# Two-layer graph network on one core: the node block's load moved behind the first feature load, and VectorE's per-tile duties moved to other tiles

## Chip, cores and metric

The kernel runs on one core of a Trainium2 chip. The metric is the device time of one execution in microseconds (us); the figure to compare is the median of the runs.

## What is computed

The graph has 6250 nodes with 256 features and 206250 edges, sorted by destination. The reference is two layers with a residual and a layer norm around each (cut to what matters here):

```python
# layer 0: every edge sends from src to dst
msg = concat([x[src], edge_attr_64]) @ W_message
agg = segment_sum(msg, dst)
h   = layer_norm(relu(agg) + x)
y   = relu_mlp_skip(h, [W0, W1, W2], [b0, b1, b2])
x1  = norm(x + layer_norm(x + y))
# layer 1: attention over the edges of one src
h      = lrelu(x1 @ w_W + w_b)
edge_h = lrelu(edge_attr_128 @ ew_W + ew_b)
e_ij   = concat([h[src], h[dst], edge_h]) @ a_W + a_b
alpha  = softmax of e_ij over the edges of one src
out    = norm(x1 + lrelu(segment_sum(alpha * h[dst], src)))
```

## The kernel before

After a short stage that prepares tables, the first long stage is a loop of 51 passes that ends near 2900 us of the span; the second long stage, the attention over sorted records, is not touched. The change concerns the pass loop alone.

One pass works on 32 tiles (numbered `kk` = 0 to 31) of 128 edges. For each tile TensorE multiplies the 128 edge features by `w_edge` (line 657) into a PSUM bank that ScalarE has filled with the bias beforehand (`seed`, line 801), and VectorE reduces the bank to one logit per edge (`edge`, line 1034). ScalarE seeds tile `kk + 3` while at tile `kk`, and a bank can be seeded only when VectorE has read the tile that used it before, four or five tiles back (nine for the fifth bank). TensorE asks for two seeds at every even tile.

Beside that, each pass carries four other jobs, spread over its tiles:

- **Segment sums of layer 0.** GpSimd gathers node rows with 35 indirect transfers (line 624, in eight batches that `picked` indexes), VectorE builds one-hot matrices `hot` (`one_hot`, line 1060), TensorE adds them up from tile 3 to tile 30 (line 672), and VectorE takes the sum at tile 30 (`take_sums`, line 1068).
- **The node block.** One block of 128 nodes goes through layer 0's dense part. `x_blk` is loaded by SyncE's queue (`load_x`, line 591), VectorE adds it (line 1090), the three MLP layers alternate between TensorE (line 731) and VectorE (lines 1107 and 1109, tiles 12, 15 and 18), two norms follow (tiles 21 to 25), `last_norm` writes `x1` as `u_n` (line 1128, tile 25), TensorE turns it at tile 28 (line 723) and multiplies it at tile 30 (`hidden`, line 751), and VectorE makes the table row from that (`table`, from line 1134, tile 30).
- **Sorting the edges by src,** for layer 1. VectorE computes ranks, writes one-hot `slot` matrices in four parts (`slots`, line 995) and `tagged` values: three parts from the keys (`tag_keys`, line 1006) in this pass and three from the logits (`tag_logits`, line 1024) at tiles 0 to 2 of the next. TensorE sorts from tile 4 of that next pass (line 696).
- **Loads.** SyncE's queue loads edge features in eight pieces of four tiles into two halves of `feats` (line 600) and 64-wide edge rows (line 604). A feature piece waits until the half's four tiles of earlier use are multiplied.

Each engine runs its own instructions in the order in which they are written, so the tile at which a duty stands in `body` sets what is queued behind it. At a pass's start SyncE first calls `load_x`, which waits for the `x1` of the previous pass.

Of the kernel before, what the change touches and what calls it, by code (L numbers as in the profile page):

```python
# [58 lines left out]
def build(nc, a, n_nodes, n_edges):  # L59
# [24 lines left out]
    with ExitStack() as top:  # L84
# [25 lines left out]
        def wait_alone(eng, *waits):  # L110
            waits = [(on, eng.to_reg(count)) for on, count in waits]
            eng.wait_ge(opened, 1)
            for on, count in waits:
                eng.wait_ge(on, count)


        def in_pairs(t):
            return t.rearrange("p t (c w) -> p t c w", w=2)

        def pairs_over(row, many):  # L120
            pairs = row.rearrange("p (c w) -> p c w", w=2)
            return pairs.unsqueeze(1).to_broadcast([P, many, row.shape[1] // 2, 2])

        def over_pairs(two, wide):
            return two.unsqueeze(2).to_broadcast([P, two.shape[1], wide // 2, 2])
# [37 lines left out]
        with ExitStack() as ctx:  # L163
# [70 lines left out]
            @block.sync  # L234
            def _(sp):
                sp.dma_start(dst_g[:], a["dst_groups"]).then_inc(idx_in, 16)
                sp.dma_start(dst_i[:], a["dst"]).then_inc(idx_in, 16)
                sp.dma_start(hi_i[:], a["src"]).then_inc(idx_in, 16)
                sp.dma_start(src_i[:], a["src"][:, 0:NTA]).then_inc(idx_in, 16)

                sp.wait_ge(blank_ready, 1)
                for n in range(2):
                    sp.dma_start(recs[n * SPAN:(n + 1) * SPAN, :].rearrange("(p t) w -> p (t w)", p=P), blank[:]).then_inc(blanked, 16)
                sp.wait_ge(blanked, 2 * 16)
# [213 lines left out]
        with ExitStack() as ctx:  # L458
# [96 lines left out]
            def count_of(eng):  # L555
                return eng.value_load(passes[0:1, 0:1], min_val=EP, max_val=NPM - 1)

            def block_at(eng, p):
                return eng.value_load(block_i[:, bass.ds(p, 1)], min_val=0, max_val=NB)

            def tile_at(eng, p):
                return eng.value_load(tile_i[:, bass.ds(p, 1)], min_val=0, max_val=USED)

            def edges_at(eng, p):
                return eng.value_load(edges_i[:, bass.ds(p, 1)], min_val=0, max_val=EP + 1)

            @block.sync
            def _(sp):
                def load(dst, src):
                    sp.dma_start(dst, src).then_inc(w_in, 16)  # L570

                load(w_edge[:, 0:D], a["ew_W"])
                for n, name in enumerate(("a_tgt", "a_nbr", "a_edge")):
                    load(row[name], a["a_W"][n:n + 1, :].to_broadcast([P, D]))
                for name in ("w_b", "ew_b", "aggr_scale", "aggr_bias", "out_scale", "out_bias"):
                    load(row[name], a[name].to_broadcast([P, D]))
                load(ab_col[:], a["a_b"].to_broadcast([P, 1]))
                for c in range(KC):
                    load(w_msg[:, c, :], a["W_message"][c * P:(c + 1) * P, :])
                    load(w_node[:, c, :], a["w_W"][c * P:(c + 1) * P, :])  # L580
                    for n in range(3):
                        load(w_mlp[:, n, c, :], a[f"mlp_W{n}"][c * P:(c + 1) * P, :])
                load(w_msg[0:DE0, KC, :], a["W_message"][D:D + DE0, :])
                for n in range(3):
                    load(b_mlp[:, n, :], a[f"mlp_b{n}"])

                def load_x(p):

                    sp.wait_ge(nx["x1"], p)
                    d = block_at(sp, p)  # L590
                    sp.dma_start(x_blk[:], a["x"][bass.ds(d * P, P), :]).then_inc(nx["x"], 16)

                n = count_of(sp)
                with sp.Fori(0, n) as p:
                    load_x(p)
                    e = edges_at(sp, p)
                    t0 = tile_at(sp, p)
                    for c in range(TILES // EB):
                        sp.wait_ge(o["y_ready"], p * TILES + (c * EB - EB + Y0))
                        sp.dma_start(feats[:, c % 2 * EB * P:(c % 2 + 1) * EB * P],  # L600
                                     a["edge128"][:, bass.ds(e * (TILES * P) + c * EB * P, EB * P)]).then_inc(f_in[c % 2], 16)
                        j, at = c, STARTS[c]
                        sp.wait_ge(o["summed"], p * NB_SUMS + (j + 1))
                        sp.dma_start(rows[:, at:at + SUMS[j], D:W0], a["edge64"][:, bass.ds(t0 + at, SUMS[j]), :]).then_inc(e_in[j], 16)
                load_x(n)
                wait_alone(sp, (nx["tab_out"], n * 16 + 16))

# [287 lines left out]
            def _(dve):  # L895
# [95 lines left out]
                def slots(p, n):  # L991
                    if n == 0:
                        wait_alone(dve, (o["ranked"], p * 2 + 2), (o["sorted"], p * U + U))
                    tiles = slice(n * SLOT_TILES, (n + 1) * SLOT_TILES)
                    v.tensor_tensor(in_pairs(slot[:, tiles, :]), pairs_over(one_up[:], SLOT_TILES), over_pairs(rank_two[:, tiles, :], P),
                                    ALU.is_equal).then_inc(o["slot_ready"], 1)
# [5 lines left out]
                def tag_keys(p, n):  # L1002

                    if n == 0:
                        wait_alone(dve, (o["keys_ready"], p + 1), (o["hb_ready"], p + 1), (o["sorted"], p * U + U))
                    v.tensor_tensor(in_pairs(tagged[:, :, n, 0, :]), in_pairs(hb[:]), over_pairs(key_two[:, n, :, :], NBP), ALU.mult)
# [16 lines left out]
                def tag_logits(w, n):  # L1023
                    ins = v.tensor_tensor(in_pairs(tagged[:, :, n, 1, :]), in_pairs(hb[:]), over_pairs(r_two[:, n, :, :], NBP), ALU.mult)  # L1024
                    if n == 2:
                        ins.then_inc(o["tagged_ready"], 1)
# [122 lines left out]
                def body(p, e, tile):  # L1149
                    at = e * TILES  # L1150
                    split_logits(p, at)
                    for kk in range(TILES):
                        edge(p, kk)
                        if kk < 3:
                            tag_logits(p, kk)
                        if kk == 3:
                            find(p, at)
                        if 4 <= kk < 7:
                            totals(p, kk - 4)
                        if kk in (7, 8):  # L1160
                            in_lane(p, kk - 7, at)
                        if kk in (9, 10):
                            up_to_here(p, kk - 9)
                        if kk in (9, 13):
                            place(p, (9, 13).index(kk), e)
                        if kk == 10:
                            key_pairs(p, at)
                        if kk in (12, 13):
                            look_up(p, kk - 12)
                        if kk == 14:  # L1170
                            halve(p)
                        if kk == 15:
                            halve_again(p)
                        if kk == 16:
                            rank_of(p)
                        if kk == 17:
                            rank_pairs(p)
                        if kk in (18, 21, 23, 27):
                            slots(p, (18, 21, 23, 27).index(kk))
                        if kk in (19, 25, 29):  # L1180
                            tag_keys(p, (19, 25, 29).index(kk))
                        if kk in hot_at:
                            one_hot(p, hot_at[kk])
                        if kk in pick_at:
                            pick(p + 1, pick_at[kk], tile)
                        if kk in node:
                            node[kk](p)
                        if kk == 24:
                            base_of(p + 1)
                            go_on(p)  # L1190
                        if kk == 25:
                            local(p + 1, tile)
                        if kk == 26:
                            one_hot(p + 1, 0)
                        if kk == 28:
                            one_hot(p + 1, 1)
                        if kk == 30:
                            take_sums(p)
# [635 lines left out]
```

## Time and profile before

| | |
|---|---|
| median of 3 runs | 5291.64 us (5288.85 to 5291.9) |
| the profiled execution: time, span | 5291.46 us, 5289.7 us |
| mean granted TensorE clock | 0.892 |
| TensorE matmul / VectorE / GpSimd busy | 74% / 67% / 68% |
| the pass loop | 51 passes; the VectorE instruction that opens a pass starts at 208.7 us the first time |

The profiled execution's span is 1.8 us under its time. Shares of busy time are means over two stages with different limits; the loop is read below from its own rows.

### The profile page before, as it was taken

What the parts mean: (1) busy time and instruction counts of PE and PEld (TensorE: products, weight loads), DVE (VectorE), ACT (ScalarE), POOL (GpSimd) and SP (SyncE); (2) the same over time, 40 slices, a digit from 0 to 9 for tenths busy, and PEclk for the clock granted to TensorE, in tenths of its full rate; (3) what the DMA queues carried; (4) which work ended last, traced back from release to release, by engine and by line L of the source; (5) the groups of instructions that cost most, each with busy time, mean ns of one, the idle gap of its engine ahead of it and who ended that gap; (6) DMA issues with size and microseconds to landing.
All of it is one profiled execution on the core that took longest, in us unless ns stands there. A gap on an engine that the chain in (4) does not pass through costs nothing. (4 is left out here: it accounts for less than half of the span.)

```text
span 5289.7 us, 86818 instructions
## 1 busy us (share of the span) xinstructions
PE 3902.5 (74%) x18662; PEld 2967.3 (56%) x18663; DVE 3563.6 (67%) x11443; ACT 1726.2 (33%) x5121; POOL 3584.2 (68%) x3655
## 2 busy tenths in 40 slices
PE   4498989898989898988887366666666666666661
PEld 3366666666666666666665255555555555555551
DVE  8778888888888888888786455555555555555554
ACT  0133333232323333333332133333333333333334
POOL 0377776777777777777773277777777777777772
PEclk9799999999999999999998688888888888888886
DMA  1356555555555555555556334344444334433343
GB/s 44 96 164 170 158 164 154 165 155 161 157 162 157 160 157 160 157 162 160 157 164 94 101 107 106 106 106 106 106 106 106 106 106 105 107 106 106 106 105 64
DMA packets 544286, 679.76 MB, mean 129 GB/s; under 512 B 340246, under 2 KB 376430, under 8 KB 543996
## 3 DMA queue, kind: packets, MB, share of 16 engines
q0 software_dynamic: 174144, 469.02, 32.6%
q1 hardware_dynamic: 355132, 196.63, 13.8%
q10 hardware_dynamic: 14976, 13.69, 0.8%
q8 instruction: 18, 0.29, 0.0%
q14 instruction: 16, 0.13, 0.0%
HBM read 650.32 MB, written 27.79 MB: 128 GB/s over the span
## 5 line engine op out<-in xcount | busy, mean ns | idle before, releaser
L624 POOL DMA_INDIRECT rows<-in_x,picked x1785 | 1799.1, 1008 | 724.1 <-issue 686.0
L1499 POOL DMA_INDIRECT room<-nodetab,nbr_idx x1736 | 1643.8, 947 | 562.4 <-issue 490.2
L672 PE MATMUL bank<-rows,hot 128*128 128x320 f32 x3570 | 1237.5, 446 | 25.7 <-DMA rows<-in_edge 19.7
L657 PE MATMUL bank<-w_edge,feats 128*128 128x258 f32 x3264 | 1050.6, 411 | 213.0 <-DMA feats<-in_edge 108.7
L801 ACT COPY bank<-b_edge 128x258 f32<-128x258 f32 x1635 | 602.7, 377 | 1460.6 <-DVE unused L1034 1442.9
L1529 PE MATMUL bank<-room,w 128*128 128x258 f32 x3472 | 1037.9, 462 | 51.2 <-ACT w L1575 50.7
L1561 ACT ACTIVATE w<-off,logit 128x128 f32<-128x128 bf16 x1736 | 534.0, 388 | 1361.0 <-DVE logit L1613 1361.0
L1529 PEld LDWEIGHTS bank<-room,w 128*128 128x128 f32 x3472 | 802.8, 238 | 244.4 <-ACT w L1575 95.0
L1520 PE MATMUL bank<-ident,w 128*128 128x128 f32 x1736 | 307.4, 330 | 777.2 <-ACT w L1561 777.2
L657 PEld LDWEIGHTS bank<-w_edge,feats 128*128 128x128 f32 x3264 | 578.7, 200 | 433.3 <-ACT bank L801 197.6
L1034 DVE SCALAR_TENSOR_TENSOR unused<-bank,a_relu 128x258 bf16<-128x258 f32 x1632 | 687.5, 421 | 199.2 <-PE bank L657 173.6
L672 PEld LDWEIGHTS bank<-rows,hot 128*128 128x128 f32 x3570 | 704.7, 198 | 179.9 <-issue 41.9
L1520 PEld LDWEIGHTS bank<-ident,w 128*128 128x128 f32 x1736 | 233.3, 166 | 824.0 <-ACT w L1561 437.0
L1618 DVE TENSOR_REDUCE best<-bank 128x1 f32<-128x896 f32 x248 | 270.7, 1091 | 475.0 <-PE bank L1520 474.9
L1613 DVE TENSOR_TENSOR logit<-r_at,room 128x7 f32<-128x7 f32 x248 | 42.4, 171 | 455.4 <-DMA room<-nodetab,nbr_idx 454.6
L1608 DVE TENSOR_SCALAR off<-iota_bf,lane_f 128x128 bf16<-128x128 bf16 x1736 | 337.8, 276 | 1.6 <-issue 1.6
L696 PE MATMUL bank<-tagged,slot 128*128 128x300 bf16 x1664 | 283.5, 293 | 54.9 <-DVE tagged L1024 54.6
L1637 DVE TENSOR_TENSOR w<-w,bank 128x896 f32<-128x896 f32 x248 | 268.5, 1083 | 58.2 <-PE bank L1512 55.3
L1060 DVE TENSOR_TENSOR hot<-iota,rel 128x512 f32<-128x512 f32 (+1 forms) x410 | 300.8, 734 | 0.1
L696 PEld LDWEIGHTS bank<-tagged,slot 128*128 128x128 bf16 x1664 | 159.4, 98 | 198.6 <-issue 143.0
L1575 ACT ACTIVATE w<-w 128x896 f32<-128x896 f32 x248 | 231.7, 934 | 4.4 <-DVE w L1637 4.4
L617 POOL DMA_INDIRECT recs<-out_rows,at_now x106 | 107.3, 1012 | 111.9 <-ACT out_rows L815 80.9
(316 smaller groups left out, 3871.4 us busy)
## 6 DMA issues: line engine op xcount, KB each, us to landing
feats<-in_edge SPq DMA_DIRECT2D x408, 256.0 KB, 2.9
rows<-in_edge SPq DMA_DIRECT2D x255, 128.0 KB, 3.0
rows<-in_x,picked POOLq DMA_INDIRECT x1785, 2.9
room<-nodetab,nbr_idx POOLq DMA_INDIRECT x1736
rows<-in_edge SPq DMA_DIRECT2D x153, 160.0 KB, 3.4
nodetab<-tab ACTq DMA_DIRECT2D x52, 129.0 KB, 2.7
x_blk<-in_x SPq DMA_DIRECT2D x52, 128.0 KB, 2.1
x_rows<-u_n ACTq DMA_DIRECT2D x52, 128.0 KB, 2.3
```

The lines of the kernel that those rows point to most:

```text
L624: pool.indirect_dma_start(out=rows[:, STARTS[j] + s, 0:D], out_offset=None, in_=a["x"], in_offset=bass.IndirectOffsetOnAxis(ap=picked[j][: ...
L657: mm(y, feats[:, f0 * P:(f0 + 1) * P], w_edge[:], start=False, stop=True, skip_group_check=True).then_inc(o["y_ready"], 1)
L672: ins = mm(S_PS, hot[j % HR][:, s - STARTS[j], :], rows[:, s, :], start=(s == 0), stop=(s == SA - 1), skip_group_check=True)
L696: ins = mm(SORT, slot[:, at, :], tagged[:, at, :, :, :].rearrange("p n f b -> p (n f b)"), start=(t == 0), stop=(t == L - 1), skip_group_c ...
L801: s.copy(logits_of(kk), b_edge[:]).then_inc(o["seeded"], 1)
L1034: v.scalar_tensor_tensor(unused[:, kk % EB, :], logits_of(kk), 0.0, a_relu[:], ALU.max, ALU.mult, accum_out=r_cur[:, kk:kk + 1]).then_inc( ...
L1060: v.tensor_tensor(hot[j % HR][:, 0:SUMS[j], :], iota[:].unsqueeze(1).to_broadcast(shape), rel[:, at:at + SUMS[j]].unsqueeze(2).to_broadcas ...
L1499: pool.indirect_dma_start(out=nbr[:, u * GC + k, :], out_offset=None, in_=nodetab, in_offset=bass.IndirectOffsetOnAxis(ap=nbr_idx[u][:, k: ...
L1520: ins = nc.tensor.transpose(T_PS[u % 2][:, k * P:(k + 1) * P], w[:, u * GC + k, :], ident[:])
L1529: ins = mm(O_PS[u % 2][:, 0:HW], w[:, u * GC + k, :], nbr[:, u * GC + k, :], start=(k == 0), stop=(k == GC - 1))
L1561: ins = s.activation(w[:, u * GC + k, :], off[:, u * GC + k, :], ACT.Identity, bias=logit[u][:, k:k + 1])
L1608: v.tensor_scalar(off[:, u * GC + k, :], iota_bf[:], lane_f[:, bass.ds(tile0(i, u) + k, 1)], MASKED, ALU.not_equal, ALU.mult)
```

## The change

It does two things. In SyncE's queue `load_x(p)` moves from the head of the pass to behind the pass's first feature and row transfers. On VectorE the same instructions stand at other tiles: `slots` at 18, 21, 26, 28 (before 18, 21, 23, 27), `tag_keys` at 17, 20, 25 (before 19, 25, 29), `base_of` and `go_on` at 22 (before 24), `local` at 23 (before 25), and the next pass's first two `one_hot` at 24 and 27 (before 26 and 28). No instruction is added or taken away.

```diff
                 with sp.Fori(0, n) as p:
-                    load_x(p)
                     e = edges_at(sp, p)
                     t0 = tile_at(sp, p)
                     for c in range(TILES // EB):
...
                         sp.dma_start(rows[:, at:at + SUMS[j], D:W0], a["edge64"][:, bass.ds(t0 + at, SUMS[j]), :]).then_inc(e_in[j], 16)
+                        if c == 0:
+                            load_x(p)
                 load_x(n)
...
-                        if kk in (18, 21, 23, 27):
-                            slots(p, (18, 21, 23, 27).index(kk))
-                        if kk in (19, 25, 29):
-                            tag_keys(p, (19, 25, 29).index(kk))
+                        if kk in (18, 21, 26, 28):
+                            slots(p, (18, 21, 26, 28).index(kk))
+                        if kk in (17, 20, 25):
+                            tag_keys(p, (17, 20, 25).index(kk))
...
-                        if kk == 24:
+                        if kk == 22:
                             base_of(p + 1)
                             go_on(p)
-                        if kk == 25:
+                        if kk == 23:
                             local(p + 1, tile)
-                        if kk == 26:
+                        if kk == 24:
                             one_hot(p + 1, 0)
-                        if kk == 28:
+                        if kk == 27:
                             one_hot(p + 1, 1)
```

The changed kernel's lines below the first edit are numbered one higher, so L1109 of before is L1110 there.

VectorE, tiles 17 to 19 of a pass, before: the logit of tile 17 (L1034), the rank pairs, the logit of tile 18, a quarter of `slot`, the residual of MLP layer 2 (L1109), the logit of tile 19, and then the first `tag_keys` (L1006).

```order
L1034 SCALAR_TENSOR_TENSOR unused,r_cur<-bank,a_relu 128x258
L987 COPY rank_two<-rank 128x64
L1033 REGISTER_ALU
L1034 SCALAR_TENSOR_TENSOR unused,r_cur<-bank,a_relu 128x258
L995 TENSOR_TENSOR slot<-one_up,rank_two 128x1024
L1109 SCALAR_TENSOR_TENSOR h_t<-bank,b_mlp,h_t 128x128 x2
L1033 REGISTER_ALU
L1034 SCALAR_TENSOR_TENSOR unused,r_cur<-bank,a_relu 128x258
L1006 TENSOR_TENSOR tagged<-hb,key_two 128x32x50
L1057 REGISTER_ALU
L1060 TENSOR_TENSOR hot<-iota,rel 128x512
```

The same place in the changed kernel:

```order
L1035 SCALAR_TENSOR_TENSOR unused,r_cur<-bank,a_relu 128x258
L988 COPY rank_two<-rank 128x64
L1007 TENSOR_TENSOR tagged<-hb,key_two 128x32x50
L1034 REGISTER_ALU
L1035 SCALAR_TENSOR_TENSOR unused,r_cur<-bank,a_relu 128x258
L996 TENSOR_TENSOR slot<-one_up,rank_two 128x1024
L1110 SCALAR_TENSOR_TENSOR h_t<-bank,b_mlp,h_t 128x128 x2
L1034 REGISTER_ALU
L1035 SCALAR_TENSOR_TENSOR unused,r_cur<-bank,a_relu 128x258
L1058 REGISTER_ALU
L1061 TENSOR_TENSOR hot<-iota,rel 128x512
```

The first `tag_keys` now stands ahead of the residual of layer 2 and not behind it.

VectorE from the logit of tile 25 to `x1` (L1128), before:

```order
L1034 SCALAR_TENSOR_TENSOR unused,r_cur<-bank,a_relu 128x258
L1006 TENSOR_TENSOR tagged<-hb,key_two 128x32x50
L1040 REGISTER_ALU
L1041 ISA
L1041 COPY picked<-src_i 128x4
L1084 REGISTER_ALU
L1085 RECIPROCAL rstd<-std 128x1
L111 REGISTER_ALU
L1128 TENSOR_SCALAR u_n<-u,mv,rstd 128x256
```

In the changed kernel, from the logit of tile 24 to `x1` (L1129 there):

```order
L1035 SCALAR_TENSOR_TENSOR unused,r_cur<-bank,a_relu 128x258
L1061 TENSOR_TENSOR hot<-iota,rel 128x640
L1034 REGISTER_ALU
L1035 SCALAR_TENSOR_TENSOR unused,r_cur<-bank,a_relu 128x258
L1007 TENSOR_TENSOR tagged<-hb,key_two 128x32x50
L1041 REGISTER_ALU
L1042 ISA
L1042 COPY picked<-src_i 128x4
L1085 REGISTER_ALU
L1086 RECIPROCAL rstd<-std 128x1
L111 REGISTER_ALU
L1129 TENSOR_SCALAR u_n<-u,mv,rstd 128x256
```

The tag there is now the third, not the second, and the next pass's first one-hot (L1061) stands ahead of it.

SyncE's queue at the head of a pass, before: the node block's load with its register load, then the two other register loads, then the first features.

```order
L559 TENSOR_LOAD pass_tab
L559 ISA x2
L591 ISA
L591 DMA x_blk<-in_x 128x256
L565 ISA
L565 TENSOR_LOAD pass_tab
L565 ISA x2
L562 ISA
L562 TENSOR_LOAD pass_tab
L562 ISA x2
L599 ISA
L600 ISA
```

In the changed kernel:

```order
L599 ISA
L599 DMA feats<-in_edge 128x512
L602 ISA
L603 ISA
L603 DMA rows<-in_edge 128x5x64
L559 ISA
L559 TENSOR_LOAD pass_tab
L559 ISA x2
L591 ISA
L591 DMA x_blk<-in_x 128x256
L598 REGISTER_ALU
L599 ISA
```

The wait for `x1` (the ISA row of L559) and the node block's transfer now stand behind the first features and rows.

## Rows read from the trace of the kernel before

**Rows 1.** Waits, 500 to 2500 us: total us, times, longest.
```profile
PE bank L657 <- DMA feats<-in_edge: 73.6, 38, 3.0
DVE h_t L1109 <- PE bank L731: 15.2, 39, 0.4
```

**Rows 2.** Timeline of VectorE, tiles 15 to 18: start, us, line, [idle before].
```profile
1024.85 0.61 DVE L1107 SCALAR_TENSOR_TENSOR h_t<-bank,b_low,s_t 128x128 f32<-128x128 f32 x2 [1.59 <-PE bank L731]
...
1027.81 0.69 DVE L995 TENSOR_TENSOR slot<-one_up,rank_two 128x1024 bf16<-128x1024 bf16 x1
1028.88 0.61 DVE L1109 SCALAR_TENSOR_TENSOR h_t<-bank,b_mlp,h_t 128x128 f32<-128x128 f32 x2 [0.39 <-PE bank L731]
```

**Rows 3.** Timeline of VectorE, tile 25 to the next pass's opening.
```profile
1039.34 0.99 DVE L1006 TENSOR_TENSOR tagged<-hb,key_two 128x1600 bf16<-128x1600 bf16 x1
1040.24 0.16 DVE L1041 COPY picked<-src_i 128x4 int32 x1
...
1040.57 0.41 DVE L1128 TENSOR_SCALAR u_n<-u,mv,rstd 128x256 f32<-128x256 f32 x1
1040.90 0.37 DVE L1048 TENSOR_SCALAR rel<-dst_f,base_cur 128x35 f32 x1
1041.46 0.43 DVE L1034 SCALAR_TENSOR_TENSOR unused<-bank,a_relu 128x258 bf16<-128x258 f32 x1 [0.19 <-DVE rel L1048]
...
1041.82 0.82 DVE L1060 TENSOR_TENSOR hot<-iota,rel 128x640 f32<-128x640 f32 x1
1042.55 0.42 DVE L1034 SCALAR_TENSOR_TENSOR unused<-bank,a_relu 128x258 bf16<-128x258 f32 x1
...
1046.25 0.42 DVE L1134 TENSOR_TENSOR u<-bank,row_w_b 128x256 f32<-128x256 f32 x1
...
1051.59 0.19 DVE L1014 TENSOR_TENSOR r_rest<-r_cur 128x32 f32<-128x32 f32 x1 [1.88 <-issue]
```

**Rows 4.** Timeline of TensorE, tiles 28 to 30 and the next pass's 0 to 3.
```profile
1039.91 0.70 PE L657 MATMUL bank<-w_edge,feats 128*128 128x258 f32 x2 [0.47 <-ACT bank L801]
...
1041.04 0.44 PE L723 MATMUL bank<-ident,u_n 128*128 128x128 f32 x2
...
1042.67 0.70 PE L657 MATMUL bank<-w_edge,feats 128*128 128x258 f32 x2 [0.22 <-ACT bank L801]
...
1043.75 1.13 PE L751 MATMUL bank<-w_node,h_t 128*128 128x256 f32 x4
...
1047.61 1.13 PE L657 MATMUL bank<-w_edge,feats 128*128 128x258 f32 x4 [2.30 <-DMA feats<-in_edge]
1050.01 2.09 PE L657 MATMUL bank<-w_edge,feats 128*128 128x258 f32 x4 [1.27 <-ACT bank L801]
```

**Rows 5.** Timelines of SyncE's queue and ScalarE there; the seeds are tiles 3 and 4.
```profile
1041.82 0.34 SPq L591 DMA_DIRECT2D x_blk<-in_x  x1
1044.06 0.33 SPq L600 DMA_DIRECT2D feats<-in_edge  x1
...
1049.58 0.68 ACT L801 COPY bank<-b_edge 128x258 f32<-128x258 f32 x2
```

**Rows 6.** Windows around two pass heads: busy us of each engine, granted clock, DMA.
```profile
1724.00:1738.00 14.00, 7.74 (x34) 5.08 (x34) 11.26 (x38) 3.70 (x11) 10.87 (x11) 1.00 0.72 208
1045.00:1059.00 14.00, 10.26 (x36) 6.95 (x35) 11.21 (x37) 3.33 (x10) 10.65 (x12) 0.76 0.73 206
```

**Rows 7.** Timelines: openings of two later passes (VectorE), TensorE's first sort between.
```profile
1731.56 0.19 DVE L1014 TENSOR_TENSOR r_rest<-r_cur 128x32 f32<-128x32 f32 x1 [1.83 <-issue]
...
1736.50 0.69 PE L696 MATMUL bank<-tagged,slot 128*128 128x300 bf16 x4 [1.93 <-DVE tagged L1024]
...
1783.86 0.19 DVE L1014 TENSOR_TENSOR r_rest<-r_cur 128x32 f32<-128x32 f32 x1 [1.81 <-issue]
```

**Rows 8.** Timelines: opening after the pass of rows 3, and GpSimd's wait in a pass.
```profile
1103.87 0.19 DVE L1014 TENSOR_TENSOR r_rest<-r_cur 128x32 f32<-128x32 f32 x1 [1.83 <-issue]
...
1014.13 0.95 POOL L624 DMA_INDIRECT rows<-in_x,picked  x1 [4.04 <-issue]
```

## The prediction

> **What bounds the kernel now.** I read the waits first, then one pass on each engine, then the same place in other passes. The waits between 500 and 2500 us, 38 passes, show TensorE waiting 73.6 us for features: 1.9 us at every pass's head, because the feature load stands behind the node block's load in SyncE's queue [rows 1, 4, 5]. They also show VectorE waiting for TensorE ahead of the MLP's layer 2: 15.2 us, 0.39 us a pass [rows 1].
>
> Which of these sets the pass? One pass lasts 1103.87 - 1051.59 = 52.28 us from opening to opening [rows 3, 8]. VectorE waits 1.59 us for layer 1 at 1024.85 and 0.39 us for layer 2 at 1028.88 [rows 2]. After 1028.88 it waits for nobody: up to the opening of the next pass at 1051.59 it has only short gaps for its own results (0.19 us before the logit of tile 26) and the 1.88 us of the loop's own turn [rows 3]. It then makes the logit tags, and TensorE's first sort waits for them, 1.93 us in the pass of rows 7. From that sort TensorE runs densely until layer 2 (the waits list no wait of its own in that stretch, and VectorE is the one that waits). So the cycle is: VectorE from layer 2's residual to the logit tags, then TensorE from the first sort to layer 2. A wait counts only if it lies on that cycle.
>
> The feature wait does not. TensorE's multiply of tiles 0 and 1 starts at 1047.61; the one of tiles 2 and 3 starts at 1050.01 whatever happened before it, as it waits for ScalarE's seed of tile 3, which ends at 1049.58 + 0.38 (half of the 0.68 us pair, its second copy being tile 4's) [rows 4, 5]. That seed stands behind ScalarE's duty for the table, which waits for VectorE. And behind tiles 2 and 3 there is one more wait for VectorE, the sort's.
>
> The clock is a second candidate. In the pass head at 1045 to 1059 us the granted clock is 0.76 on average, so 0.24/0.5 x 14 = 6.7 us were at the lower level, 1.2 GHz: four matmuls took 2.09 us there, against 1.13 at the higher level, 2.4 GHz [rows 4, 6]. But another head, 1724 to 1738 us, had 1.00 throughout, and its pass took 1783.86 - 1731.56 = 52.30 us, the same; the sort merely waited 1.93 us [rows 6, 7].
>
> **The change, part by part.**
>
> *SyncE's queue.* The first features now wait only for tile 27's multiply and not for `x1`. Before, `x_blk` is issued at 1041.82, the features at 1044.06, and they are used at 1047.61, 3.55 us later [rows 4, 5]. Tile 27 is multiplied before 1039.91 minus the 0.47 us wait, so the features are issued near 1039.5 at the latest and there by 1043.1, ahead of 1047.61 - 2.30 = 1045.31, when TensorE asks. The feature wait, 1.9 us, goes. What is late next is the seed of tile 3: TensorE does tiles 0 and 1 about 1.7 us earlier and then waits so much longer. Worth: 0 us on the cycle. The seed wait and the sort wait are the cover; were both gone it would be worth up to 1.9 us a pass. `x_blk` itself leaves when `x1` is there, as before, and is wanted only at tile 5 of the next pass; queued behind it are the second features, which wait for tile 31 anyway (near 1045.3). One register load fewer stands before the first features, and none is added.
>
> *VectorE, the tag at tile 17.* A `tag_keys` takes 1040.24 - 1039.34 = 0.90 us in the stream [rows 3]. Moved ahead of layer 2's residual, it fills the wait there. A `slot` quarter takes 0.69 - 0.09 = 0.60 us in the stream (the tag's own row overlaps its follower by the same 0.09), so before, VectorE could have gone on at 1027.81 + 0.60 = 1028.41 and went on at 1028.88: 0.47 us were idle [rows 2]. With the tag ahead the residual starts at 1028.41 + 0.90 = 1029.31, which is 0.43 us later, and everything behind it finds 0.90 us less in front. Net: 0.47 us a pass earlier. TensorE doesn't want that residual until tile 21.
>
> *The other moves.* The second tag goes from 25 to 20, the third from 29 to 25, two `slot` quarters one to three tiles later, `base_of`, `go_on`, `local` and two one-hots earlier. All of them stay between the residual and `table`, where VectorE has no idle time to fill, so their sum is 0 us as long as nothing in that stretch begins to wait. Three places could:
> - `x1` comes later. Between residual and `x1` there are still two tags, but `local` (1041.46 - 1040.90 = 0.56 us) and a 640-wide one-hot (1042.55 - 1041.82 = 0.73) replace a `slot` quarter (0.60): +0.69 us, with the residual's 0.43 +1.1 us, so `x1` starts at 1041.7 and not 1040.57 [rows 3].
> - TensorE turns `x1` 0.47 us after that start (1041.04 against 1040.57), and `hidden` ended at 1043.75 + 1.13 = 1044.88, 3.84 us after the turn. In this lies a wait for a seed ahead of tile 30 (0.22 us idle at 1042.67) that a later `x1` swallows: 3.6 us remain, and `hidden` ends at 1041.7 + 0.47 + 3.6 = 1045.8 [rows 3, 4].
> - `table` wants `hidden`. It started at 1046.25 and would now be free to start at 1046.25 - 0.47 = 1045.78 [rows 3]. So nothing is left, within my 0.2 us of reading. If `hidden` is late by 0.2 us, nearly half the gain goes; I take it as late by 0 to 0.1.
>
> Seeds for tiles 28 and 29 also come later, as logits 24 and 25 do: TensorE's 0.47 us wait at tile 28 grows to about 1.5 us [rows 4]. It is off the cycle: it is inside the chain through `x1` just counted.
>
> *Sum.* 0.47 us in about 50 of 51 passes: 23.5 us. The second stage is unchanged. I take off 4 us for passes in which the clock falls at a worse place than now (below): 19.5 us. On the profiled execution's 5291.46 us (its span 5289.7 and 1.8 around it; 0.2 us under the median of the runs, 5291.64) that is **5272 us**.
>
> **The skill's rule.** The row shows that a clock fall follows the idle time at the pass head, and that a pass without one is no shorter [rows 6, 7]. The Trainium skill, "TensorE: Matmul & The Clock Gate", section "HAM oscillation — how this bites in real kernels", says that a wait for a transfer in every round of a loop puts TensorE back to the slow clock each time and that the cost is the slow time times one half. By that rule the load's move alone would return 6.7 x 0.5 = 3.4 us of such a pass. That is the first rival.
>
> **The rivals.**
> 1. *The feature wait and the clock count after all* (chance 0.10). If TensorE's head were on the cycle, 1.9 us a pass would come back, 95 us, and up to 3.4 us more with the clock. But GpSimd then becomes the bound: it waits 4.04 us a pass now [rows 8], so no pass can get shorter by more than that. Time: 5197, at the very least 5090. Against it stand the two passes of equal length with and without slow clock.
> 2. *No measurable change* (0.24). `hidden` is late for `table` by 0.3 us or more, or a logit in the stretch behind the residual, where VectorE had nothing to wait for, now waits. Each takes 0.2 to 0.4 us of the 0.47. Time: 5291.5 - 50 x 0.1 = 5286.
> 3. *Slower: the clock falls in the dense stretch* (0.09). Now it falls in the head, where half speed costs nothing, as two waits cover it. With TensorE working steadily at tiles 31, 0 and 1 the fall can miss the head and come at the wait for the sort, 1.93 us long when the clock is full [rows 7], and so reach into the stretch behind the sort, which is on the cycle. Half speed for the 6.7 us of rows 6, of which 3 to 5 behind the sort, costs 1.5 to 2.5 us in such a pass. It decides from about one pass in four (0.25 x 2 = 0.5 against 0.47). In every second pass it would give 5291.5 + 50 x (1.0 - 0.47) = 5318. For it: the sum of idle time stays, so a fall has to come somewhere. Against it: the seed wait of about 2.5 us stays in the head and is longer than the sort's wait. I expect one or two such passes in fifty: the 4 us above.
>
> **How the numbers follow.** The forecast case, a gain of 0.3 to 0.5 us a pass, has 0.57: 5264 to 5280. A measurement of this kernel can tell about 0.2%, 10.6 us, from no change. Below 5281 lie the forecast and rival 1: 0.67. Between lies rival 2: 0.24. Above lies rival 3: 0.09. The range leaves out rival 1 and most of rival 3; it goes from 5254 (0.75 us a pass, should a part of the head's 1.9 us count) to 5290.
>
> **What the changed profile would show.** The wait of TensorE for the features is gone; its wait for ScalarE before tiles 2 and 3 is near 2.6 us. VectorE's wait before layer 2's residual (L1110) is gone; the one at layer 1 is still near 1.6. Pass openings are 51.8 us apart. The wait at tile 28 is near 1.5 us. `table` (L1135) has no wait for TensorE; one there is rival 2. Windows behind the first sort have the clock at 1.00; below that is rival 3. The prediction is wrong if openings are 50 us apart or less, or more than 52.3.

## The result and the profile after

The changed kernel takes 5319.97 us, the median of 12 runs (5299.84 to 5366.29), against 5291.45 (5283.25 to 5293.06) for the kernel before. The ratio estimated from the runs is 1.0066, 95% interval 1.0047 to 1.0085 (the medians alone give 1.0054). It is slower, and its runs spread over 66 us where those of before spread over 10. The profiled execution is the fastest of the twelve, 5299.84 us with a span of 5298.1.

Waits of the changed kernel between 500 and 2500 us (total us, times, longest):

```profile
PE bank L658 <- ACT bank L802: 181.6, 97, 2.8
DVE h_t L1108 <- PE bank L732: 71.3, 70, 1.6
PE bank L697 <- DVE tagged L1025: 63.6, 37, 1.9
DVE u L1091 <- PE bank L719: 63.4, 38, 3.5
```

TensorE's wait for the features is gone from the list, and so is VectorE's wait ahead of layer 2's residual (L1110): neither row of [rows 1] is left. A wait that was short has grown: VectorE ahead of the node block's first sum (L1091), tile 5, 63.4 us and up to 3.5 at a time. Before the change the same view showed for it

```profile
DVE u L1090 <- PE bank L718: 22.9, 38, 0.6
```

One pass of the changed kernel that went as forecast, timeline of VectorE (start, us, line, idle before):

```profile
1158.04 0.19 DVE L1015 TENSOR_TENSOR r_rest<-r_cur 128x32 f32<-128x32 f32 x1 [2.04 <-issue]
1166.78 0.42 DVE L1091 SCALAR_TENSOR_TENSOR u<-bank,x_blk 128x256 f32<-128x256 f32 x1 [0.60 <-PE bank L719]
1183.63 0.61 DVE L1108 SCALAR_TENSOR_TENSOR h_t<-bank,b_low,s_t 128x128 f32<-128x128 f32 x2 [1.59 <-PE bank L732]
1188.09 0.61 DVE L1110 SCALAR_TENSOR_TENSOR h_t<-bank,b_mlp,h_t 128x128 f32<-128x128 f32 x2
1204.47 0.42 DVE L1135 TENSOR_TENSOR u<-bank,row_w_b 128x256 f32<-128x256 f32 x1
1209.88 0.19 DVE L1015 TENSOR_TENSOR r_rest<-r_cur 128x32 f32<-128x32 f32 x1 [1.95 <-issue]
```

And TensorE in it, at tile 28 and at tiles 2 and 3 of the next pass:

```profile
1199.73 0.70 PE L658 MATMUL bank<-w_edge,feats 128*128 128x258 f32 x2 [1.50 <-ACT bank L802]
1208.23 2.09 PE L658 MATMUL bank<-w_edge,feats 128*128 128x258 f32 x4 [2.80 <-ACT bank L802]
```

It lasts 1209.88 - 1158.04 = 51.84 us, 0.44 less than the 52.28 of before. L1110 waits for nobody, L1108 still waits 1.59, `table` (L1135) has no wait, tile 28 waits 1.50 us and tiles 2 and 3 wait 2.80 for their seed.

Two passes that follow each other are not like it, on VectorE:

```profile
1261.64 0.19 DVE L1015 TENSOR_TENSOR r_rest<-r_cur 128x32 f32<-128x32 f32 x1 [1.90 <-issue]
1273.20 0.42 DVE L1091 SCALAR_TENSOR_TENSOR u<-bank,x_blk 128x256 f32<-128x256 f32 x1 [3.41 <-PE bank L719]
...
1316.26 0.19 DVE L1015 TENSOR_TENSOR r_rest<-r_cur 128x32 f32<-128x32 f32 x1 [1.95 <-issue]
1327.82 0.42 DVE L1091 SCALAR_TENSOR_TENSOR u<-bank,x_blk 128x256 f32<-128x256 f32 x1 [3.42 <-PE bank L719]
...
1370.86 0.19 DVE L1015 TENSOR_TENSOR r_rest<-r_cur 128x32 f32<-128x32 f32 x1 [1.92 <-issue]
```

The head of the first of them in windows (length; busy us of PE, PEld, DVE, ACT, POOL; granted clock; DMA share, GB/s):

```profile
1256.00:1265.00 9.00, 5.02 (x21) 3.23 (x19) 6.20 (x26) 2.11 (x6) 6.87 (x8) 1.00 0.84 208
1265.00:1267.00 2.00, 0.41 (x2) 0.28 (x3) 2.00 (x7) 1.11 (x4) 1.70 (x2) 0.65 0.52 141
1267.00:1272.00 5.00, 5.00 (x16) 3.27 (x13) 2.79 (x8) 0.48 (x2) 3.78 (x5) 0.50 0.30 93
1272.00:1280.00 8.00, 8.00 (x40) 5.60 (x40) 5.67 (x24) 2.77 (x9) 1.14 (x2) 0.97 0.29 79
```

And TensorE at its first sort:

```profile
1266.59 1.18 PE L697 MATMUL bank<-tagged,slot 128*128 128x300 bf16 x4 [1.93 <-DVE tagged L1025]
1267.56 1.07 PE L658 MATMUL bank<-w_edge,feats 128*128 128x258 f32 x2
```

These passes last 54.62 and 54.60 us, 2.8 more than the one above. The whole head, with its 2.8 us wait, runs at the full clock (1.00 up to 1265). The clock falls while TensorE waits for the tags, between 1265 and 1267, and stays at the lower level, 1.2 GHz, through the first 5.9 us of the dense stretch behind the sort (0.4 us up to 1267, 5.0 up to 1272, and 0.03/0.5 x 8 = 0.5 behind it): the sort's four matmuls take 1.18 us against 0.69 in [rows 7], a tile's product 1.07 against 0.60 to 0.70. VectorE waits 3.41 us for its first node sum where it waited 0.60: 2.8 us more, which is all that the pass is longer by. In the next pass it happens again at the same place, 54.6 us later.

From opening to opening, 48 passes (the second to the 49th) take 2529.5 us in this profile against 2510.3 before. 32 of them average 51.81 us; 14 last 54.5 to 54.8 and two 53.0 and 53.2. In the heads of 25 of the 48 passes the clock falls before the sort, and these passes last 51.80 us on average; in 16 it falls at the sort (the long ones and the two of 53 us); in seven it doesn't fall at all, and they last 51.84. The last pass, in which TensorE waits for transfers, took 67.6 us against 76.4.

### The profile page after: what moved, and what is told of

Read it like the earlier page. It is cut to its first block and busy times, and to the rows that moved or that the text cites. A ratio compares the mean times of both kernels' runs of the same rounds, so it can differ in the third digit from the quotient of the medians.

```text
span 5298.1 us, 86767 instructions
## 1 busy us (share of the span) xinstructions
PE 3866.7 (73%) x18662; PEld 2967.8 (56%) x18663; DVE 3553.6 (67%) x11443; ACT 1735.2 (33%) x5121; POOL 3561.3 (67%) x3655
## 5 line engine op out<-in xcount | busy, mean ns | idle before, releaser
L625 POOL DMA_INDIRECT rows<-in_x,picked x1785 | 1765.4, 989 | 767.1 <-issue 618.7
L658 PE MATMUL bank<-w_edge,feats 128*128 128x258 f32 x3264 | 1007.9, 399 | 254.4 <-ACT bank L802 232.0
L1035 DVE SCALAR_TENSOR_TENSOR unused<-bank,a_relu 128x258 bf16<-128x258 f32 x1632 | 686.5, 423 | 190.4 <-PE bank L658 165.3
L697 PE MATMUL bank<-tagged,slot 128*128 128x300 bf16 x1664 | 299.0, 305 | 79.4 <-DVE tagged L1025 79.3
L1061 DVE TENSOR_TENSOR hot<-iota,rel 128x512 f32<-128x512 f32 (+1 forms) x410 | 302.8, 739 | 0.1
```

The source lines that it names most:

```text
L625: pool.indirect_dma_start(out=rows[:, STARTS[j] + s, 0:D], out_offset=None, in_=a["x"], in_offset=bass.IndirectOffsetOnAxis(ap=picked[j][: ...
L658: mm(y, feats[:, f0 * P:(f0 + 1) * P], w_edge[:], start=False, stop=True, skip_group_check=True).then_inc(o["y_ready"], 1)
L697: ins = mm(SORT, slot[:, at, :], tagged[:, at, :, :, :].rearrange("p n f b -> p (n f b)"), start=(t == 0), stop=(t == L - 1), skip_group_c ...
L1035: v.scalar_tensor_tensor(unused[:, kk % EB, :], logits_of(kk), 0.0, a_relu[:], ALU.max, ALU.mult, accum_out=r_cur[:, kk:kk + 1]).then_inc( ...
L1061: v.tensor_tensor(hot[j % HR][:, 0:SUMS[j], :], iota[:].unsqueeze(1).to_broadcast(shape), rel[:, at:at + SUMS[j]].unsqueeze(2).to_broadcas ...
```

## The experiments

Theory 1 is the prediction's third rival: a clock fall at the sort's wait makes the long passes, and VectorE's order gives 0.47 us in the others. Theory 2: VectorE's new order itself makes the long passes. Theory 3: the features' wait was on the cycle. Beside them stood two more: any low clock costs time, and transfers make the long passes. The first four kernels ran on one chip beside a before of 5289.12 us.

**One half of the change at a time.** Only SyncE's queue:

```diff
-                    load_x(p)
...
+                        if c == 0:
+                            load_x(p)
```

> Only the move of the node block's load; VectorE's order is that of before. Theory 1 (a clock fall behind the first sort): a normal pass stays at 52.3 us, as VectorE's order is unchanged and the features are off the cycle; but TensorE's idle time moves towards the sort, so some passes have their clock fall there and last about 2.9 us more, 55.2. With 5 to 12 such passes: 5305 to 5326 us. Theory 2 (the new order on VectorE alone makes the slow passes): 5291, no slow pass. Theory 3 (the feature wait was on the cycle): under 5250.

It took 5281.62 us, ratio 0.9985 (0.9976 to 0.9994). No pass is long: 48 average 52.28. The guess that falls would come to the sort was wrong here; with VectorE's old order TensorE's wait in the head is 3.8 us long, 47 falls come in 49 heads, and none between the sort and tile 5. What it gains, 7.5 us by the medians, lies in the last two passes, 123.3 us together in its profile against 133.3 in that of before. Theory 3 falls too: without the feature wait a normal pass is no shorter.

Only VectorE's order, with the load at the head:

> Only VectorE's new order; the node block's load leads the pass as before. Theory 1: normal passes at 51.8 us, and TensorE's wait for the features stays in the pass head, so that the clock falls there and not at the sort: 0 to 3 slow passes, 5268 to 5277 us, faster than before. Theory 2: as many slow passes of 54.7 us as in the changed kernel, 5300 to 5366 us.

5264.0 us, ratio 0.9954 (0.9941 to 0.9968), no long pass, 48 passes at 51.79. So neither half is slow alone. VectorE's half gives what the prediction worked out, and in these profiles the long passes come only with both halves (one single long pass of a later run stands against this, below). Its waits show what stands in the head instead:

```profile
PE bank L657 <- DMA feats<-in_edge: 98.4, 39, 3.0
PE bank L657 <- ACT bank L801: 69.6, 58, 1.5
```

2.5 us a pass for the features, as `x1` and the load behind it come later. Falls come in the head in 32 of 48 passes and nowhere later; the passes with one average 51.80 us, those without 51.78.

**Filling the head's wait.** The changed kernel with matmuls whose results nobody reads:

```diff
+                def fill(many):
+                    for _ in range(many):
+                        mm(banks[4][:, 0:D + 2], ones[:], w_edge[:], start=True, stop=True, skip_group_check=True)
...
                     for kk in range(TILES):
+                        if kk == 2:
+                            pe.wait_ge(o["rows_ready"], p * U + U)
+                            fill(5)
                         edge(p, kk)
```

> The changed kernel, and five more matmuls of 128x258 (results are thrown away) ahead of tile 2, in TensorE's 2.8 us wait for the seed. Theory 1: the clock can no longer fall in the head, so it falls at the sort's wait more often: at least as many slow passes of 54.7 us as in the changed kernel, 5320 to 5400 us. A theory by which low clock anywhere costs time, or by which added TensorE work costs time: with the first, faster than the changed kernel as there is less slow clock; with the second, each normal pass is longer than 51.8.

5272.03 us, ratio 0.9969 (0.9958 to 0.998): faster than the changed kernel, where theory 1 in my form said at least as slow. The trace says why. All 13 falls of the 48 passes come at the sort and none in the head, as expected; but they are no more than in the changed kernel's profiles (16 and, below, 32). Each lasts less of the dense stretch, so the long passes last 53.3 us and not 54.7, and they don't come in a row: 2 to 4 short passes, 51.65 us on average, lie between two of them. Windows around one (its opening is at 682.26):

```profile
682.00:686.50 4.50, 2.49 (x11) 1.37 (x9) 4.05 (x14) 1.17 (x4) 3.59 (x4) 1.00 0.81 206
686.50:691.00 4.50, 3.94 (x14) 2.75 (x15) 3.90 (x11) 1.18 (x4) 3.28 (x5) 0.62 0.33 96
691.00:696.00 5.00, 5.00 (x25) 3.35 (x24) 2.81 (x12) 0.98 (x3) 1.79 (x2) 1.00 0.33 90
```

About 3.4 us of the 4.5 after 686.5 are at the lower level ((1.00 - 0.62)/0.5 x 4.5), against some 6.9 in the changed kernel's long pass at 1261.64 (1.4, 5.0 and 0.5 in its last three windows). All of the 3.4 us lies behind the sort, which starts at 687.06 while the clock falls near 687.4; of the 6.9 us, 5.9 lie behind it. Half of that is 1.7 and 2.9 us, and the passes are longer by 1.6 and 2.8: behind the sort the half speed costs its full price. So where exactly the fall comes matters twice: for what one costs, and for whether it comes again.

**Filling both waits.** The same, and three more between tile 4's sums and the first sort:

```diff
+                        if kk == 4:
+                            fill(3)
```

> As the run with five added matmuls ahead of tile 2, and three more of the same between tile 4's sums and the first sort, in TensorE's 1.9 us wait for VectorE's tags. Theory 1: the clock never falls in a pass, all passes last 51.8 us, and the time is 5266 to 5272 us with a spread as small as that of before. Rival: if the long passes come from something else (transfers, VectorE's order), they stay: 5300 us or more.

5248.35 us, ratio 0.9924 (0.991 to 0.9937), with runs from 5245.3 to 5250.3. Its window over 2000 us:

```profile
500.00:2500.00 2000.00, 1865.11 (x9006) 1407.39 (x9005) 1627.59 (x5696) 630.48 (x1894) 1430.34 (x1438) 1.00 0.59 162
```

The same window of the kernel before:

```profile
500.00:2500.00 2000.00, 1802.00 (x8313) 1314.84 (x8312) 1616.31 (x5623) 617.08 (x1874) 1431.50 (x1420) 0.96 0.56 160
```

The clock is 1.00 throughout and was 0.96, and all 48 passes average 51.66 us. No transfer was changed, and the long passes are gone. It beats the expected 5266 by 18 us. The expectation had left out the last pass (66.8 us in this profile against 76.4 before) and the first one (56.8 against 58.3), together 11 us; the other 7 are passes of 51.66 us where it had 51.8. Why the passes with fills are a little shorter than fall-free ones without fills (51.78 and 51.84 above) was not looked for.

**Filling the sort's wait alone.**

```diff
                         if kk == 4:
+                            pe.wait_ge(o["rows_ready"], p * U + U)
+                            fill(3)
```

(and no fill at tile 2)

> The changed kernel with the three added matmuls before the first sort alone, none ahead of tile 2. If the long passes come from a clock fall in the sort's wait, filling that wait removes them though the head's wait of 2.8 us and its falls stay: no pass of 54.7 us, nearly all at 51.8, 5256 to 5266 us. Passes with slow clock in the head may be up to 1 us longer, as the added work takes twice as long there. Rival (any long wait of TensorE in the head leads to long passes): slow passes stay, 5290 us or more.

5260.06 us against a before of 5291.52 on its chip, ratio 0.994 (0.9926 to 0.9954). 37 falls in 49 heads, all before the sort; no pass of 54 us or more. 44 of the 48 passes average 51.67 us, the same for the 32 of them with a fall in the head and the 12 without. The other four last 52.8 to 53.1: in them the slow stretch begins 2.2 to 2.5 us ahead of the opening and lasts into the added matmuls ahead of the sort, as the expectation had feared. So the head's 2.8 us wait is harmless, and so is slow clock that ends before the sort; the fall in the wait at the sort made the long passes.

**The changed kernel once more,** for a second profile on the same chip.

> The changed kernel once more, for a second profile. Its runs spread from 5300 to 5366 us. If the spread is the number N of long passes, this execution's time is near 5252 + 2.9 x N, with N counted from its own trace, and the other passes last 51.8 us.

5342.47 us. 31 passes of 54.5 to 54.8 us, one of 53.2, the other 16 average 51.81: 5252 + 2.9 x 31 = 5342. VectorE in two long passes that follow each other:

```profile
1026.89 0.19 DVE L1015 TENSOR_TENSOR r_rest<-r_cur 128x32 f32<-128x32 f32 x1 [1.87 <-issue]
1038.46 0.42 DVE L1091 SCALAR_TENSOR_TENSOR u<-bank,x_blk 128x256 f32<-128x256 f32 x1 [3.42 <-PE bank L719]
1081.52 0.19 DVE L1015 TENSOR_TENSOR r_rest<-r_cur 128x32 f32<-128x32 f32 x1 [1.95 <-issue]
```

The stretches from the end of the head, in windows:

```profile
1030.00:1038.00 8.00, 6.16 (x18) 3.88 (x18) 5.04 (x14) 1.59 (x5) 5.99 (x6) 0.57 0.41 118
1084.00:1092.00 8.00, 6.07 (x18) 3.54 (x17) 5.66 (x16) 1.97 (x6) 6.18 (x7) 0.59 0.45 125
```

In this profile 18 long passes follow one another, then come nine that are not of their length, two long ones, five others and 11 long ones. Behind a long pass the next is long 28 times of 31, behind another 3 of 16; in the first profile it is 10 of 14 and 4 of 33. Every fall of a long pass of 54 us or more comes 3.8 to 4.1 us behind the opening, in both profiles. Once such a fall has made a pass 54.6 us long, the next mostly comes at the same place again. The sum fits both profiles, so the spread of the twelve runs is most likely the number of passes caught in such rows; the other eleven runs have no trace that could show it.

**Which of VectorE's moves gives the 0.47 us.** The kernel before with its first tag at tile 17:

```diff
-                        if kk in (19, 25, 29):
-                            tag_keys(p, (19, 25, 29).index(kk))
+                        if kk in (17, 25, 29):
+                            tag_keys(p, (17, 25, 29).index(kk))
```

> The kernel before with a single edit: the first tag_keys at tile 17, not 19. By the prediction's sum this one move fills VectorE's wait before layer 2's residual and is the whole gain of VectorE's new order: passes of 51.8 us, 5262 to 5270 us, the same as the run with all of VectorE's new order (5264). If the other moves carry part of it, the gain is smaller, 5275 or more.

5290.46 us, ratio 0.9995 (0.9986 to 1.0004): nothing. The waits:

```profile
DVE unused L1034 <- PE bank L657: 126.2, 268, 1.1
DVE h_t L1107 <- PE bank L731: 74.6, 76, 1.6
PE bank L696 <- DVE tagged L1024: 41.7, 35, 1.9
DVE u L1090 <- PE bank L718: 22.8, 38, 0.6
```

The wait ahead of layer 2's residual is gone, but VectorE now waits 0.53 us more for a product at tile 21, since tile 19 became shorter by the tag and TensorE is not there yet: 126.2 us for logits where the kernel before has 105.5. The logit of tile 21, before and here:

```profile
1031.81 0.43 DVE L1034 SCALAR_TENSOR_TENSOR unused<-bank,a_relu 128x258 bf16<-128x258 f32 x1
1032.84 0.43 DVE L1034 SCALAR_TENSOR_TENSOR unused<-bank,a_relu 128x258 bf16<-128x258 f32 x1 [0.52 <-PE bank L657]
```

Then two edits, the second tag at tile 20 as well:

```diff
-                        if kk in (19, 25, 29):
-                            tag_keys(p, (19, 25, 29).index(kk))
+                        if kk in (17, 20, 29):
+                            tag_keys(p, (17, 20, 29).index(kk))
```

> The kernel before with tag_keys at 17, 20 and 29, once more, since on the chip of the first try even the kernel before took 6664 us. If the gain of VectorE's new order needs work in both places: passes of 51.8 us, 5262 to 5270 us. If the later moves carry it: 5285 or more.

5268.69 us against 5291.2, ratio 0.996 (0.9946 to 0.9974); 47 passes average 51.90, and the wait at tile 21 is gone. So these two moves together give nearly the whole gain, and the first alone gives none of it; the second alone was not run. One pass is long, 54.8 us with its fall 4.0 us behind the opening, though the node block's load leads the queue here: a single long pass doesn't need the load's move; rows of them were seen only with both halves. A first try of this kernel and of the last one below fell on a chip on which the kernel before took 6663.67 us; there this kernel took 6622.42 (ratio 0.9935, 0.9919 to 0.9952) and the other 6643.04 (0.9968, 0.9954 to 0.9982), so that on that chip the last one is the slower of the two. The expectation on record for that try:

> The kernel before with two edits: tag_keys at 17, 20 and 29, not 19, 25 and 29. The first tag alone gave nothing: VectorE's wait ahead of layer 2's residual was gone and a wait of 0.5 us stood at the logit of tile 21. If the gain of VectorE's new order needs work in both places, this version has it whole: passes of 51.8 us, 5262 to 5270 us. If the later moves (slots, local, one-hots) carry it, it stays at 5285 or more.

**More work ahead of the waits.** The kernel with both fills, and:

```diff
-                        if kk == 16:
+                        if kk == 15:
                             rank_of(p)
-                        if kk == 17:
+                        if kk == 16:
                             rank_pairs(p)
-                        if kk in (18, 21, 26, 28):
+                        if kk in (18, 20, 26, 28):
-                        if kk in (17, 20, 25):
+                        if kk in (16, 17, 21):
...
-                hot_at = {SUM_KK[j - 2] + 1: j for j in range(2, NB_SUMS)}
+                hot_at = {SUM_KK[j - 2] + (0 if j == 5 else 1): j for j in range(2, NB_SUMS)}
```

> The kernel with both fills, and more of VectorE's work moved ahead of its waits for TensorE: rank_of and one one-hot ahead of layer 1's residual (1.59 us wait), rank pairs and the first two tags at tiles 16 and 17, the third tag at 21. If VectorE's stretch from the middle of the pass to the next sort is still the cycle's half, the third tag (0.9 us) leaves the dense tail and a pass lasts 50.8 us: 5203 to 5215 us. Rival: VectorE now only waits for TensorE's products at tiles 18 to 22 in place of its old waits, and the pass stays at 51.7: 5245 or more.

5238.07 us, ratio 0.9899 (0.9884 to 0.9914); passes average 51.35 us, 0.31 less than with both fills and not the 0.9 of a tag. The waits name what ended it:

```profile
DVE unused L1044 <- PE bank L658: 116.1, 272, 1.1
DVE h_t L1117 <- PE bank L732: 18.2, 73, 0.3
DVE u L1144 <- PE bank L752: 14.9, 39, 0.4
```

The wait at layer 1 is filled (72.7 us before this step, 18.2 now), and VectorE waits for `hidden` ahead of `table` (L1144): the wait of the prediction's second rival, 0.38 us a pass. The waits for logits have grown too, from 105.7 us with both fills to 116.1, 0.27 us a pass. With the 0.31 gained these two make about the tag's 0.9. With `hidden` one tile sooner:

```diff
-                        28: turn_x1, 30: hidden}
+                        28: turn_x1, 29: hidden}
-                        29: take_x1, 31: take_p}
+                        28: take_x1, 31: take_p}
```

> The version with more work moved earlier and hidden at tile 29, once more for the same reason. If hidden is what holds that version: passes of 51.0 us, 5216 to 5224 us. If another wait takes its place: 5230 or more.

5229.93 us against 5291.2, ratio 0.9886 (0.987 to 0.9903): the fastest version here. Its waits no longer name L752; passes average 51.03 us as expected. The time is 6 us above the expected range all the same. The last two passes take 132.3 us in its profile, against 128.8 in the version that it starts from and 122.8 with both fills; that is 3.5 us of it, and its profiled execution was the fastest of its four, 5226.83, while that of the version before was the slowest of four. The rest wasn't followed up. The expectation on record for its first try:

> The version with more work moved earlier, and hidden at tile 29 instead of 30 on TensorE, take_x1 at 28 instead of 29 on ScalarE. That version's VectorE waits 0.38 us a pass for hidden ahead of table. If hidden is what holds it, the wait goes and a pass lasts 51.0 us: 5216 to 5224 us. If the two bound each other closely (another wait takes its place at the logit of tile 30 or 31), 5230 or more.

## Why the prediction was wrong

The mechanism of the normal pass was right. Openings came 51.8 us apart as forecast; L1110's wait went, L1108's stayed at 1.59, tile 28 waits 1.50, the seed wait is 2.80 (2.6 forecast), `table` doesn't wait. VectorE's half alone gave 25 us of the forecast 23.5, and the features' wait was worth nothing in a normal pass, as said: 52.28 us with it and without. One step there was wrong: the tag at tile 17 was given the whole gain and the other moves 0. Alone it gives nothing, as a logit behind the residual begins to wait, which is a form of the second rival; the second tag at tile 20 fills the wait that the first one leaves behind. That the sum of 0.47 us held is luck in this: the second tag happened to be moved as well. (Two slips of calculation, half of 0.68 as 0.38 and 5286.5 as 5286, change nothing.)

The step that failed is the one behind "I take off 4 us for passes in which the clock falls at a worse place": rival 3, with a chance of 0.09. The prediction had the place (the sort's wait), what brings it about (a busier head) and a cost of 1.5 to 2.5 us a pass, from 3 to 5 us of slow clock behind the sort; it was 5.9 us, and the long passes cost 2.8. It sized how often at "one or two such passes in fifty", and it was 16 in one profile and 32 in another. The 48 passes took 43 and 89 us more in these profiles than 48 of 51.81 us would have, where the sum has 4.

Two things were missing. The argument against was that the head's wait is the longer one and would catch the falls. It does in 25 of 48 passes in one profile and in 12 of 48 in the other. And it took falls as independent of each other, but they come in rows, up to 18 long passes one behind the other, all with the fall at the same place. The likely reason is that a fall at the sort sets the length of its pass to 54.6 us, and that at this length the next one meets the same place; the passes of 53.3 us with the filled head don't come in rows. No experiment changed the length of a pass alone, so the reason stays argued. With 0.47 x 48 = 23 us gained, 9 us gained in the last pass and 2.9 lost in each long pass, the break-even is at 11 of 50 passes; the 12 runs lie above it. The rival's own time for every second pass, 5318 us, is near the measured 5320 by luck: its long pass costs 2 us and not 2.8, and it has no gain in the last pass.

That last gain, 7 to 9 us in the pass that waits for transfers, was in no term either. From about 2834 us to the loop's end TensorE waits 26.5 us for edge rows and features before, and 15.6 with the load alone moved. With `x_blk` behind them the last pass took 66.8 to 69.3 us in the profiles (71.8 in the fastest version), and 74.2 to 77.4 in three of four with `x_blk` ahead. It took 69.5 in the fourth, so the load's place isn't the whole cause; what else plays a part stays open.

The Trainium skill's rule, "TensorE: Matmul & The Clock Gate", section "HAM oscillation — how this bites in real kernels", that repeated waits bring the slow clock back each round, is borne out in most rounds: the clock falls in 45 of 48 heads before and in 32 of 48 with VectorE's half alone. What it makes of the time, half of the slow time, holds behind the sort (2.9 us for 2.8 measured, above) and not in the head. VectorE's half alone has a granted clock of 0.98 from 500 to 2500 us, so 0.02/0.5 x 2000 = 80 us of slow clock, all in the heads; by the rule, as an estimate, 40 us of that would come back. With no slow clock at all (both fills) its 48 passes are 6.6 us shorter, 2479.6 against 2486.2, and even that isn't the clock's, as its passes with and without a fall are equally long. The cost depends on whether the slow stretch lies on the cycle.

Left open: why the falls of the changed kernel leave the head in some passes and come to the sort, while with VectorE's half alone, whose head wait begins about 0.9 us earlier, they leave it as well in 16 of 48 passes and never come to the sort. The prediction's own reason for such falls, that a fall has to come somewhere, isn't borne out: in those 16 passes, and in seven of the changed kernel's, none comes. That the distance between the two waits decides was not tried.

## What to carry to other kernels

- A wait off the critical path can be doing work: here TensorE's waits in the pass head held the slow clock in a place where it cost nothing. Before shortening such a wait ask where the clock will fall then, and look at the waits that stand right before the dense stretch.
- A stall that lengthens a round can repeat in round after round. The chance of one fall times its cost is then the wrong sum; look for rounds of one and the same longer length, and for runs that spread.
- Moving work into one wait pays only as far as the next place where the engine would wait; fill them in order, and read the waits again after each.

## What the runs showed of the hardware

- Matmuls whose results are thrown away, 8 per pass of 0.43 us each, kept the granted clock at 1.00 for 2000 us, where it was 0.96 in the kernel before. They made the kernel 72 us faster than the changed one by the medians, and 53 us faster between the two profiled executions, of which the changed one's had 16 long passes.
- A slow stretch of about 3.4 us of the clock behind the sort lengthened the pass by 1.6 us (to 53.3), one of about 6.9 by 2.8 (to 54.6), of which 1.0 lies in the wait itself. With the sort's wait filled, 32 passes with slow clock in the head and 12 without lasted 51.67 us both.
- On one chip the kernel before took 6663.67 us, 26% more, at a mean granted clock of 0.81 where it has 0.89 elsewhere. In the profile of the version with two tags on that chip 48 passes averaged 69.5 us, while one logit on VectorE took 0.42 us there as here; the cause was not looked for.
